# Attention masks by four 64x64 tiles of the array, and the transpose of the row maximum ahead of them

## The reference, cut to what matters

```python
x = x + _L0_xattn_ref(_layernorm(x), ctx, ctx, ...)   # 16 heads of 8, band |q - k| <= 64
x = x + _L0_ffn_ref(_layernorm(x), ...)
x = x + _L1_xattn_ref(...); x = x + _L1_ffn_ref(...)
x = x + _L2_xattn_ref(..., mask)                       # 16 heads of 8, mask from the inputs
x = x + _L2_ffn_ref(...)
x = x + _L3_xattn_ref(...)                             # 16 heads of 64, causal
x = x + _L3_ffn_ref(...)
# each of the three: softmax(q k^T * scale, masked) v, then the output projection
```

## Time and profile before

| | us |
|---|---|
| median of 3 runs | 2579.67 |
| lowest, highest | 2577.32, 2589.92 |
| the profiled execution | 2582.87 |
| its span (first to last instruction) | 2581.1 |
| TensorE busy | 2211.9 (86%) |
| VectorE, ScalarE, GpSimd busy | 1246.5, 920.6, 513.5 |

### The profile page before, as it was taken

The page is one execution under the profiler, slowest core; times in us unless marked ns, Lnnn a source line. Parts: engine busy times, 40 slices in busy tenths (PEclk is TensorE's granted clock), DMA queues, the critical chain, the costliest instruction groups (busy, mean ns, idle before and its releaser), DMA issues. The chain is left out here.

```text
span 2581.1 us, 48834 instructions
## 1 busy us (share of the span) xinstructions
PE 2211.9 (86%) x19312; PEld 1461.9 (57%) x19312; DVE 1246.5 (48%) x3264; ACT 920.6 (36%) x2319; POOL 513.5 (20%) x471
## 2 busy tenths in 40 slices
PE   4999954775599999799969999999989999999665
PEld 1556553663487788366545555555555666667521
DVE  4565545664412121455544444444435555555476
ACT  1333211654144444233323333233215555556200
POOL 4122102663111110222210101001002323333100
PEclk8999956876599999899979999999989999999689
DMA  4000000000000000200000000000010000000001
GB/s 132 10 10 6 2 1 20 17 5 5 0 2 2 2 1 2 83 10 11 2 2 1 1 0 0 0 0 1 1 42 5 5 5 9 5 1 2 1 0 33
DMA packets 20687, 28.21 MB, mean 11 GB/s; under 512 B 3982, under 2 KB 15254, under 8 KB 19990
## 3 DMA queue, kind: packets, MB, share of 16 engines
q1 hardware_dynamic: 20488, 25.37, 3.1%
HBM read 23.27 MB, written 2.10 MB: 10 GB/s over the span
## 5 line engine op out<-in xcount | busy, mean ns | idle before, releaser
L1701 ACT ACTIVATE arena<-quad,arena 114x512 f32<-114x512 f32 x192 | 131.1, 687 | 350.7 <-PE quad L1657 350.7
L1786 DVE SCALAR_TENSOR_TENSOR arena<-quad,arena 114x512 f32<-114x512 f32 x192 | 142.9, 750 | 219.6 <-ACT arena L1701 218.6
L508 DVE TENSOR_REDUCE arena<-pair 128x8 f32<-128x1024 f32 x128 | 156.8, 1225 | 185.3 <-PE pair L338 185.3
L1656 PE MATMUL quad<-arena,wide 128*114 128x512 f32 x384 | 204.9, 615 | 21.0 <-DVE arena L1786 21.0
L211 POOL TENSOR_TENSOR rstd<-var_eps,neg_half 128x4 f32<-128x4 f32 (+1 forms) x64 | 66.2, 1035 | 677.6 <-DVE var_eps L207 580.4
L1657 PE MATMUL quad<-arena,wide 128*114 128x512 f32 x384 | 197.1, 595 | 0.0
L1645 PEld LDWEIGHTS single<-wide,arena 114*128 114x128 f32 x1536 | 180.5, 192 | 27.4 <-issue 27.4
L2204 POOL TENSOR_TENSOR arena<-arena 128x512 f32<-128x512 f32 x128 | 130.4, 1040 | 317.1 <-DVE arena L2127 317.1
L1645 PE MATMUL single<-wide,arena 114*128 114x128 f32 x1536 | 180.6, 275 | 0.0
L590 POOL TENSOR_SCALAR arena<-arena 128x512 f32<-128x512 f32 x56 | 86.6, 1564 | 354.9 <-ACT arena L444 354.9
L1437 ACT ACTIVATE arena<-quad,arena 128x256 f32<-128x256 f32 x256 | 111.1, 475 | 107.7 <-PE quad L1366 107.5
(11 more groups left out here) (377 smaller groups left out, 4176.2 us busy)
## 6 DMA issues: line engine op xcount, KB each, us to landing
arena<-in_ctxT SPq DMA_DIRECT2D x32, 256.0 KB, 2.8
wide<-in_w SPq DMA_DIRECT2D x2, 2048.0 KB, 10.1
wide<-in_wgu SPq DMA_DIRECT2D x1, 2736.0 KB
x<-in_x SPq DMA_DIRECT2D x4, 512.0 KB, 6.1
out_x<-x SPq DMA_DIRECT2D x8, 256.0 KB, 3.6
wide<-in_w SPq DMA_DIRECT2D x1, 1368.0 KB
we<-in_we SPq DMA_DIRECT2D x1, 512.0 KB, 12.0
wide<-in_wq SPq DMA_DIRECT2D x1, 512.0 KB, 3.3
```

The source lines that it names most:

```text
L508: dve.tensor_reduce(mx[m % 2][:, 8 * p:8 * p + 8], S[:].rearrange("p (h k) -> p h k", h=8), AX.X, ALU.max).then_inc(s["s_free"], 1)
L1656: pe.matmul(bank[2 + k % 2][0:FR, :], wg[:, e, cols], xnT[u], start=True, stop=True)
L1701: act.activation(sg[0:FR, k % 2, :], bank[2 + k % 2][0:FR, :], ACT.Silu, bias=bgc[0:FR, e, f:f + 1]).then_inc(s["sg_ready"], 1)
L1786: dve.scalar_tensor_tensor(out=hid[e % 2][0:FR, f, :], in0=bank[4 + k % 2][0:FR, :], scalar=b1c[0:FR, e, f:f + 1], in1=sg[0:FR, k % 2, :], ...
```

## The change

Each mask pair goes into two banks by four matmuls, each on a quarter of the array (64 rows by 64 columns). The rows r of the array write to bank r; the quarter on the diagonal reads the mask as it is ("own"), the other reads a copy with its halves of rows exchanged ("other"). The mask is stored once, 128 wide, and read four times over by a stride of zero. The set-up makes the exchanged copies: GpSimd for the band and the causal mask, SyncE by four more loads of the mask bytes of layer 2. The band is symmetric, so both its uses share a tile. In the 8-wide heads `turn_max(n + 1)` moves ahead of both masks.

```diff
+        def mask_banks(pe, banks, masks):
+            for r in range(2):
+                rows = slice(64 * r, 64 * r + 64)
+                for c in range(2):
+                    pe.matmul(banks[r][64 * c:64 * c + 64, :], identb[rows, rows],
+                              masks[r ^ c][rows, :].unsqueeze(1).broadcast_to([64, 4, P]), start=True, stop=False,
+                              skip_group_check=True)
...
             for i in range(2):
-                sp.dma_start(mask_words[:, i, :], t["mask2"][i]).then_inc(w_in[2], 16)
+                sp.dma_start(mask_words[:, i, 0, :], t["mask2"][i]).then_inc(w_in[2], 16)
+                for h in range(2):
+                    sp.dma_start(mask_words[64 * h:64 * h + 64, i, 1, :],
+                                 t["mask2"][i, 64 - 64 * h:128 - 64 * h]).then_inc(w_in[2], 16)
...
                 def mask_scores(m, p):
                     pe.wait_ge(s["s_free"], 2 * m + p)
-                    for r in range(2):
-                        pe.matmul(S[:, r * 512:(r + 1) * 512], identb[:], maskS, start=True, stop=False,
-                                  skip_group_check=True)
+                    mask_banks(pe, [S[:, r * 512:(r + 1) * 512] for r in range(2)], mask_bias[l]["S"])
...
                     pe.wait_ge(s["st_free"], 2 * n)
-                    for r in range(4):
-                        pe.matmul(T[:, r * 512:(r + 1) * 512], identb[:], maskT, start=True, stop=False,
-                                  skip_group_check=True)
+                    for r in (0, 2):
+                        mask_banks(pe, [T[:, i * 512:(i + 1) * 512] for i in (r, r + 1)], mask_bias[l]["T"])
...
+                    if n + 1 < N:
+                        turn_max(n + 1)
                     mask_turned(n)
                     if n + 2 < N:
                         mask_scores(n + 2, 0)
-                    if n + 1 < N:
-                        turn_max(n + 1)
                     turned(n)
...
-                    for r in range(2):
-                        pe.matmul(S[o][:, r * 512:(r + 1) * 512], identb[:], maskS, start=True, stop=False,
-                                  skip_group_check=True)
+                    mask_banks(pe, [S[o][:, r * 512:(r + 1) * 512] for r in range(2)], mask_bias[3]["S"])
```

More of the change, by code:

```diff
@@ L80, in program @@
         neg_half = sb("neg_half", [P, G])
-        mask_bias = {l: [sb(f"mask{n}{l}", [P, 4, P], BF16) for n in names]
-                     for l, names in ((0, "ST"), (2, "ST"), (3, "S"))}
-        mask_words = sb("mask_words", [P, 2, P // 4], I32)
+        mask_bias = {l: {n: [sb(f"mask{n}{l}{half}", [P, P], BF16)[:] for half in ("own", "other")] for n in names}
+                     for l, names in ((0, "S"), (2, "ST"), (3, "S"))}
+        mask_bias[0]["T"] = mask_bias[0]["S"]
+        mask_words = sb("mask_words", [P, 2, 2, P // 4], I32)
         aw = {l: {n: sb(f"w{n}{l}", [P, P]) for n in "qkvo"} for l in (0, 2)}
@@ L110, in program @@
         w_in = {l: sem(f"w_in{l}") for l in range(4)}
+        w_loads = {0: 8, 2: 8 + 6}
         setup_v = sem("setup_v")
@@ L170, in load_pool @@
             pool.memset(earlier[:], 1.0)
-            for l in (0, 3):
-                for m in mask_bias[l]:
-                    pool.memset(m[:], 0.0)
+            band, band_other = mask_bias[0]["S"]
+            causal, causal_other = mask_bias[3]["S"]
+            band_lower, causal_lower = (arena.tensor[:, i * 64:i * 64 + 64].bitcast(BF16) for i in range(2))
+            for m in (band, band_other, causal, causal_other, band_lower, causal_lower):
+                pool.memset(m, 0.0)
             pool.drain()
@@ L179, in load_pool, with keep_where @@
                 pool.memset(ones_cols[:, j, 8 * j:8 * j + 8], 1.0)
[L181 to L185, removed]
-            pool.drain()
-            for m in mask_bias[0]:
-                pool.affine_select(out=m[:], in_=m[:], compare_op=ALU.is_ge, fill=NEG, base=64,
-                                   pattern=[[0, 4], [1, P]], channel_multiplier=-1)
+            def keep_where(m, base, step, rows):
+                pool.affine_select(out=m, in_=m, compare_op=ALU.is_ge, fill=NEG, base=base,
+                                   pattern=[[step, P]], channel_multiplier=rows)
+            keep_where(band, 64, -1, 1)
+            keep_where(causal, 0, -1, 1)
+            keep_where(band_other, 0, 1, -1)
+            keep_where(band_lower, 0, -1, 1)
+            keep_where(causal_other, 64, -1, 1)
+            keep_where(causal_lower, -64, -1, 1)
+            pool.drain()
+            keep_where(band, 64, 1, -1)
+            pool.drain()
+            pool.tensor_copy(band_other[64:128, :], band_lower[64:128, :])
+            pool.drain()
+            pool.tensor_copy(causal_other[64:128, :], causal_lower[64:128, :])
+            pool.drain()
             pool.affine_select(out=earlier[:].rearrange("p (e f) -> p e f", e=E),
@@ L221, in load_dve @@
                 dve.drain()
[L222 to L225, removed]
+            dve.wait_ge(w_in[2], 16 * w_loads[2])
+            for i, n in enumerate("ST"):
+                for h, m in enumerate(mask_bias[2][n]):
+                    dve.tensor_scalar(m, mask_words[:, i, h, :].bitcast(U8), -1.0, -NEG, ALU.add, ALU.mult)
             for l in (0, 2):
-                dve.wait_ge(w_in[l], 16 * (8 + (l == 2) * 2))
+                dve.wait_ge(w_in[l], 16 * w_loads[l])
                 dve.tensor_scalar(acol[l][:, 2:3], acol[l][:, 0:1], float(DH) ** -0.5, None, ALU.mult)
@@ L262, in small_heads @@
             wq, wk, wv, wo = (aw[l][n] for n in "qkvo")
-            maskS, maskT = (m[:].rearrange("p a k -> p (a k)") for m in mask_bias[l])
             bo = arow[l]
@@ L392, in attend @@
                     mm.then_inc(s["pv_ready"], 1)
-                pe.wait_ge(w_in[l], 16 * (8 + (l == 2) * 2))
+                pe.wait_ge(w_in[l], 16 * w_loads[l])
                 pe.wait_ge(s["vcol_ready"], 1)
@@ L467, in turned_max @@
                     act.activation(mts[m % 2], O[:, 256:320].bitcast(BF16), ACT.Copy).then_inc(s["mts_ready"], 1)
-                act.wait_ge(w_in[l], 16 * (8 + (l == 2) * 2))
+                act.wait_ge(w_in[l], 16 * w_loads[l])
                 act.activation(vcol, ident[:], ACT.Identity, bias=acol[l][:, 3:4], scale=0.0).then_inc(s["vcol_ready"], 1)
@@ L1863, in wide_heads @@
             ring = bank[4:8]
-            maskS = mask_bias[3][0][:].rearrange("p a k -> p (a k)")
             pieces = [(n, c) for c in range(HB) for n in "qk"] + [("v", c) for c in range(HB)]
```

## The result

| | us |
|---|---|
| before, median | 2578.49 |
| changed, median (range) of 4 | 2619.07 (2618.86 to 2620.73) |
| ratio, 95% interval | 1.0151 [1.0132, 1.0169] |
| the changed kernel's profiled execution, its span | 2619.14, 2617.4 |

The kernel became 1.5% slower. The forecast was 2591, with a range of 2573 to 2612: the direction was right, and the time lies above the range, 2 us under the rival in which the clock drops (2621).

What follows compares the result with a forecast made beforehand. TensorE's order of work was taken as the bound. 8-wide heads +16.4, 64-wide heads -6.8 and set-up +1.9 gave +11.5 us on the profiled 2582.87, so 2594.4; less 3.2 for the median, 2591 us, range 2573 to 2612.

Steps and rivals of the forecast that it cites:

- the rival in which the clock drops: 8-wide heads: new TensorE idle time halves the clock after each of 20 short batches, adding 30 us: 2621; chance 0.07.
- Column and row tiles run together in bfloat16: Mask pairs: four quarter-array matmuls overlap, two banks in 0.215 us plus 0.02 for later starts, instead of 0.43.
- A step into 64x64: Masks following 128x128 work: each change of tile shape costs 0.09 us, at 60 of 64 masks in the 64-wide heads.
- The transpose is at S+2.97: 8-wide heads: VectorE's chain lets the transpose start no earlier than 2.97 us after the previous batch's second scores start (S).
- the turned scores at S+3.91 for 3.88: Long 8-wide batches (projection or output ahead of masks): turned scores 3.88 us after S, where it was 3.50, +0.38.
- batches of 8.36 for 8.33: 8-wide heads: batches of 8.33 us throughout, 9.3 with a key projection, in place of 8.15, 7.78 and 8.74 to 9.07.
- The serial cost of the order: 8-wide heads: the transpose going first puts masks behind its wait; 8.2 us a stage, +16.4 for two, net of mask gains.
- The 64-wide heads: Mask pairs there go from 0.43 to 0.235 us, 60 of 64 paying 0.09 for shape: 6.8 us gained.
- The set-up's +1.9: Set-up: four more DMAs issued by SyncE ahead of the big weights delay the first projection by 1.9 us.
- The sum: Whole kernel: 16.4 for the 8-wide heads, less 6.8 for the 64-wide, plus 1.9 for set-up, +11.5 us.
- Its sign: 8-wide heads: a granted clock below 0.97 would show the forecast wrong.
- column tiles take turns: Rival: column tiles of one row group run in turn in bfloat16, masks cost as before; +74 us, 2654; chance 0.05.

Runs made afterwards that it cites:

- experiment 3: Against the changed kernel, 3, 5 or 7 idle float32 matmuls fill TensorE's idle time ahead of the wait for the maximum; 2589.7 us, ratio 1.0044.
- Experiment 4: Against the changed kernel, 5 or 7 idle float32 matmuls ahead of the wait, only in batches with no projection or output before the masks; 2590.4 us, ratio 1.0036.
- experiment 2: Against the kernel before, only the transpose of the maximum moved ahead of the masks, which stay full-array; 2653.1 us, ratio 1.0295.
- experiment 1: Against the changed kernel, the transpose of the maximum moved back behind both masks, quarter-array masks kept; 2553.5 us, ratio 0.9911.
- 6: Against the kernel with quarter-array masks but the old order, full-array masks again in the 64-wide heads; 2560.1 us, ratio 0.9938 to the kernel before.
- experiments 8 and 9: Six idle matmuls behind each first score of the 8-wide heads: on quarter masks, old order, ScalarE loads, 2529.8 us; on the kernel before, 2558.8 us.

## Why the prediction was right and wrong

**Right, by the row.** Column and row tiles run together in bfloat16: the four matmuls of a mask pair start 3 to 4 ns after each other and the groups 0.21 to 0.25 us apart. The Trainium skill, "TensorE: Matmul & The Clock Gate", section "Measured speedup vs the span model", gives each further tile about 4 ns; the trace agrees with it. A step into 64x64 costs 0.10 where 0.09 was said. The transpose is at S+2.97 in the long batches too, the turned scores at S+3.91 for 3.88, batches of 8.36 for 8.33, and 9.41 with a key projection for 9.3 (9.55 from turned scores to turned scores). The serial cost of the order, +16.4 by the sum, is +18.6 with the clock held (experiment 3). Most of the difference is VectorE: in the 12 batches with a query projection the transpose starts at S+3.12, not 2.97, and 0.15 x 12 = 1.8. The 64-wide heads gained 4.5 (6.8 said) with 5.7 us more of half clock; against whole-array masks under nearly the same clock they gain 6.0. The set-up's +1.9 was +1.7.

**Wrong: the clock.** The sum held TensorE's clock fixed. That step failed: the new idle time of the short batches let it drop to 1.2 GHz, 45 us more of it in the two stages. The fill takes 49 us of half clock away and gives 21.4 us back there; the rest of the 40.0 is the serial part. Of the 28 us by which the median lies above the forecast, the clock is 21.4, the serial part 2.2, and the 64-wide heads 2.3; the set-up and the stages without an edit take 1.1 off; and 3.2 is what I took off because the profiled execution of before was that much above its median, which that of the changed kernel wasn't. I had the clock as the third rival, at 2621, with a chance of 0.07. Its mechanism is the one that the runs show; that its time comes within 2 us is in part luck, because it priced 20 drops at 30 us, and the fill prices the 12 drops of the trace at 21.4. Its sign showed too: a granted clock below 0.97, which was 0.96 from 60 to 320 us. I dismissed it because the short batches of before idle for 0.4 to 0.5 us and keep full clock. But that row stands far from the 1.3 to 1.9 us that the change makes, and the row at the other end, the start of the stage, idles for over 1.3 us in a round and ran at half. Experiment 4 shows that the new idle time of the short batches was on the side of the second. I had both rows and took the mild one.

**What the runs exclude.** That the quarter tiles draw the clock down (experiment 2 has none, and loses clock; experiment 3 has them all, and doesn't), that the change of shape eats the gain (1, 6), that column tiles take turns. Open is why one idle stretch of 1.3 to 1.9 us drops the clock and the next one doesn't, and whether its length counts or the work around it: the long batches differ from the short ones in both. At the start of the second stage in experiment 1 one drop follows an idle stretch of only 0.77. The experts' stage took 381 to 396 us in these profiles, with 57 to 72 us of half clock and none, two or four stretches of "issue", with nothing changed in it. A comparison of whole times carries that in it; the times of the edited stages, with the half clock beside them, don't. The 29.4 of experiment 3 and the 23 of experiments 8 and 9 are to be read so.

## What to carry to other kernels

Before an instruction that waits is moved ahead of work, take from the trace the earliest time at which its wait can end, counted from the instruction that starts the chain; all that now stands behind it starts there, and the work that was ahead of it no longer hides anything. Halving the work that covers a wait gains only down to the end of that wait, here 0.4 of 0.65 us. And price idle time of TensorE by the clock as well: idle matmuls into a bank that is overwritten anyway are a cheap test of it, and at the start of a stage they were a gain, 7.2 and 11.9 us over two stages here. Whoever reads a gain from whole times should look at the stages without an edit first: here half of it was there.

## What the runs showed of the hardware that was not expected

Four tiles of 64x64 with bfloat16 moving data of stride zero do two banks of 512 in 0.21 to 0.25 us, against 0.43 by two whole-array matmuls. Stretches of 0.8 to 0.9 us without TensorE work, every 8.36 us, left the granted clock at 1.00 (busy 240.8 of 260); with stretches of 1.3 to 1.9 us besides, in every fourth batch and in the last ones, it fell to 0.96 over the same window. TensorE can also stand idle in the middle of a stage with no wait that the profile shows, 1.5 to 2.7 us at a time; in the experts' stage the nine kernels with such stretches had 30 to 32 loads of instructions, the two without 13.
